# One transformer block on one core: the feed-forward part's residual stream, statistics and last product laid out with tokens on partitions

## The reference, cut to what matters

```python
xn = _layernorm(x, axis=-1)
x = x + _L0_attn_ref(xn, ...) + _L0_ffn_ref(xn, ...)
...
def _layer(x, wqkv, qs, ksc, wo, lg, lb, w1, b1, w2, b2):
    h = shift_token(x)          # second half of the channels from the token before
    q, k, v = split(h @ wqkv)   # 8 heads of 64; l2norm, scales, rotation
    o = local_attention(q, k, v)             # windows of 64, looks one window back
    x = x + o @ wo
    h = shift_token(x)
    mu = h.mean(-1, keepdims=True)
    var = h.var(-1, keepdims=True)
    h = (h - mu) / jnp.sqrt(var + 1e-05) * lg + lb
    h = h @ w1 + b1             # 128 -> 2 * 341
    a, g = jnp.split(h, 2, axis=-1)
    h = a * jax.nn.gelu(g, approximate=False)
    x = x + h @ w2 + b2         # 341 -> 128
    return x
```

## Time and profile before

| what | value |
|---|---|
| three runs, median (lowest to highest) | 379.59 us (376.76 to 379.63) |
| the profiled execution's own time | 379.34 us |
| its span, first to last instruction | 377.5 us |
| mean granted TensorE clock | 0.991 of full |
| busy: PE, ACT, DVE, POOL | 91%, 76%, 71%, 66% |
| instructions | 10808 |

### The profile page before, as it was taken

One profiled execution on the slowest core, in us unless ns is written; L12 is line 12 of the kernel. 1 busy time (PEld: TensorE's weight loads), 2 busy tenths in 40 slices (PEclk: granted clock), 3 DMA queues, 4 the chain that ended last, 5 costly groups with the idle time before them and its releaser, 6 DMA issues. The chain is left out here.

```text
span 377.5 us, 10808 instructions
## 1 busy us (share of the span) xinstructions
PE 344.2 (91%) x4015; PEld 264.3 (70%) x4015; DVE 268.9 (71%) x474; ACT 285.3 (76%) x881; POOL 250.5 (66%) x242
## 2 busy tenths in 40 slices
PE   1758779999999999998998989999999999999996
PEld 0557557888888888667565667778888887666565
DVE  4636677878887888657868767878887887565544
ACT  2746378998999899888635689989899989886321
POOL 2999479999989999821015778788989898320000
PEclk9999899999999999999999999999999999999999
DMA  6986032222232222270020322232223222200011
GB/s 201 372 158 184 5 126 56 65 68 55 65 71 66 51 64 65 65 259 16 9 56 0 71 69 67 52 76 58 56 61 79 58 65 61 55 7 16 20 36 56
DMA packets 35954, 28.68 MB, mean 76 GB/s; under 512 B 19221, under 2 KB 29375, under 8 KB 35391
## 3 DMA queue, kind: packets, MB, share of 16 engines
q1 hardware_dynamic: 35615, 27.54, 27.8%
q10 hardware_dynamic: 288, 0.46, 0.4%
HBM read 9.64 MB, written 1.05 MB: 28 GB/s over the span
## 5 line engine op out<-in xcount | busy, mean ns | idle before, releaser
L1204 ACT ACTIVATE probs<-ps,neg_max 128x128 f32<-128x128 f32 x256 | 90.1, 376 | 6.2 <-DVE neg_max L1438 5.4
L641 POOL TENSOR_TENSOR qkn<-work 128x512 f32<-128x512 f32 x64 | 80.6, 1281 | 12.3 <-DVE work L1384 9.2
L655 POOL TENSOR_TENSOR probs_n<-probs,row_inv 128x512 f32<-128x512 f32 x64 | 66.9, 1045 | 21.8 <-DVE row_inv L1443 19.9
L649 POOL TENSOR_TENSOR qkn<-qkn,rnorm 128x512 f32<-128x512 f32 x64 | 65.6, 1046 | 17.0 <-ACT rnorm L1160 16.5
L1204 ACT ACTIVATION_READ_ACCUMULATOR probs<-ps,neg_max 128x1 f32 x256 | 55.1, 215 | 0.0
L1153 ACT ACTIVATE work<-ps 128x1024 f32<-128x1024 f32 x32 | 32.8, 1026 | 18.2 <-issue 12.3
L1374 DVE TENSOR_REDUCE ss_pair<-work 128x16 f32<-128x1024 f32 x32 | 39.0, 1220 | 8.2 <-ACT work L1153 6.2
L166 PE MATMUL ps<-wqkv_hi,h_hi 128*128 128x512 f32 x96 | 42.5, 442 | 1.6 <-ACT work L1153 1.6
L1438 DVE TENSOR_REDUCE neg_max<-ps 128x4 f32<-128x512 f32 x64 | 41.0, 682 | 3.3 <-PE ps L865 3.3
L1384 DVE TENSOR_TENSOR work<-ps,cos_w 128x1024 f32<-128x1024 f32 x32 | 38.7, 1210 | 2.3 <-PE ps L168 2.3
L1384 DVE TENSOR_TENSOR work<-ps,sin_w 128x1024 f32<-128x1024 f32 x32 | 38.7, 1210 | 0.0
(11 more groups left out here) (156 smaller groups left out, 731.3 us busy)
## 6 DMA issues: line engine op xcount, KB each, us to landing
v_off<-v_tok SPq DMA_DIRECT2D x64, 128.0 KB, 2.3
k_t<-k_t SPq DMA_DIRECT2D x30, 128.0 KB, 2.3
cos_w<-in_cos_t SPq DMA_DIRECT2D x2, 1024.0 KB, 7.8
sin_w<-in_sin_t SPq DMA_DIRECT2D x2, 1024.0 KB, 10.7
x<-xin SPq DMA_DIRECT2D x16, 128.0 KB, 2.4
x_shift<-x SPq DMA_DIRECT2D x64, 32.0 KB, 1.8
x_raw<-in_x SPq DMA_DIRECT2D x4, 256.0 KB, 4.6
x_shift<-in_wqkv SPq DMA_DIRECT2D x1, 768.0 KB, 8.6
```

The lines of the kernel that those rows point to most:

```text
L641: pool.tensor_tensor(to, first, second[:, :, ::-1, :], ALU.add).then_inc(rot_summed, 1)
L649: pool.tensor_tensor(of, of, rnorm[:, part * HEADS:(part + 1) * HEADS].unsqueeze(2) .broadcast_to([P, HEADS, DH]), ALU.mult).then_inc(rot_ ...
L655: pool.tensor_tensor(probs_n[:, 4 * g:4 * g + 4, :], probs[:, 4 * g:4 * g + 4, :], row_inv[:, 4 * g:4 * g + 4].unsqueeze(2).broadcast_to([ ...
L1204: e = act.activation(probs[:, k, :], s_ps[g][:, cw * P:(cw + 1) * P], ACT.Exp, bias=neg_max[:, k:k + 1], accum_out=row_sum[:, k:k + 1])
```

## The change

The residual stream, the statistics and the result of the last product are laid out with tokens on partitions. `project_out` and `feed_out` swap their two operands, so that the products come out as 128 tokens by 128 channels. `feed_out` becomes 4 groups (`q`) of products with 128 moving columns, and `feed_out_last` likewise. `b2` and the patch branch's bias are two more rows of `w2` against rows of ones. The LayerNorm's shift is taken through `w1` once, at the front (`weigh_ln_shift`, 12 products with one moving column), and added to `b1` (`shift_biases`). `centered`, `variance`, `square`, `norm_rstd`, `normalize` on VectorE, `turn_out`, `turn_out_last`, `put_out` and `put_last` go.

In their place: `tile_stats` on VectorE (mean and variance of one tile), for tile t-3 as the last thing in each step t; `span_rstd` on ScalarE on 128x4 numbers, in steps 8 and 12 and twice later; `normalize_tile` on GpSimd for tiles 0 to 11 and `normalize_last` on VectorE for the last four; `turn_normalized` on TensorE (4 transposes per span); `round_normalized` on ScalarE, which applies the gain, and a shorter `split_normalized` on VectorE. Between the layers `turn_next` (4 transposes per span) is new, `round_turned` and `split_input` read PSUM, and those of spans 2 and 3 stand ahead of steps 1 and 2. The raw input is added on GpSimd (`add_raw`). `shift_x1` becomes three DMAs per tile, `shift_next` three per span. The load of `w1` goes to another buffer, and waits for the split of layer 0's `wqkv`.

```diff
@@ SP
 def shift_x1(n, t):
-    sp.dma_start(x1_shift[0:64, cols(t * P, P)], x1[0:64, cols(t * P, P)])
-    sp.dma_start(x1_shift[64:P, cols(t * P + 1, P)], x1[64:P, cols(t * P, P)])
+    sp.dma_start(hs[:, t, 0:DIM // 2], x1_tok[:, t, 0:DIM // 2])
+    sp.dma_start(hs[1:P, t, DIM // 2:], x1_tok[0:P - 1, t, DIM // 2:])
+    if t < TILES - 1:
+        sp.dma_start(hs[0:1, t + 1, DIM // 2:], x1_tok[P - 1:P, t, DIM // 2:])
...
-sp.wait_ge(xn_tr, SPANS)
+sp.wait_ge(wqkv_split, 1)
 sp.dma_start(w1_raw, w1.rearrange("l p n -> p l n"))
@@ GpSimd
+def normalize_tile(layer, t):
+    pool.wait_ge(ln_rstd_done, SPANS * layer + span_of(t) + 1)
+    pool.tensor_scalar(xn_tok[:, t, :], hs[:, t, :], mv[:, t, 0:1], rstd0[:, t:t + 1],
+                       ALU.subtract, ALU.mult)
...
     scale_rotated(n + 1)
+    if t == TILES - 1:
+        for tile in range(4, 8): normalize_tile(layer, tile)
     for g in range(2): normalize(n, g)
+    if t == TILES - 2:
+        for tile in range(4): normalize_tile(layer, tile)
+    if t == TILES - 1:
+        for tile in range(8, 12): normalize_tile(layer, tile)
@@ TensorE
 def feed_out(layer, j):
-    for c, (at, size) in enumerate(HID_PARTS):
-        pe.matmul(ffn_ps, w2_s[0:size, layer, c, :], hidden_of(layer, j, c)[0:size, :])
+    for q in range(4):
+        to = ffn_ps[:, q * P:(q + 1) * P]
+        for c in range(len(HID_PARTS)):
+            pe.matmul(to, hidden_of(layer, j, c)[0:rows, q * P:(q + 1) * P], w2_s[0:rows, layer, c, :])
...
 turn_patch_out(0)
+weigh_ln_shift()
 project_qk(0, 1)
...
 def step(t, parity):
+    if layer > 0 and t in (1, 2):
+        pe.wait_ge(v_evac, n + 1)
+        turn_next(t + 1)
     scores(n, parity)
     project_out(n - 2)
-    if t == TILES - 2: variance(0)
...
-    if t == TILES - 3: centered(0)
-    if t == TILES - 2: centered(1)
...
 scores(last, 1)
-centered(2)
 project_out(last - 2)
-variance(1)
+turn_normalized(0)
 weigh_values(last - 1, 0)
 gates(0, 0)
 turn_probs(last, 0, True)
 turn_probs(last, 1, True)
-variance(2)
 project_out(last - 1)
 gates(0, 1)
+turn_normalized(1)
 weigh_values(last, 1)
 project_out(last)
 gates(0, 2)
+turn_normalized(2)
 gates(1, 0)
-centered(3)
 gates(1, 1)
-variance(3)
 feed_out(layer, 0)
+gates(1, 2)
+gates(2, 0)
+turn_normalized(3)
+feed_out(layer, 1)
@@ ScalarE
 def step(t, parity):
+    if layer > 0 and t in (1, 2): round_turned(t + 1)
     exps(n, 0)
...
     inverse_norms(n + 2)
-    if layer > 0 and t in (1, 2): round_input(t + 1)
+    if t in (8, 12): span_rstd(t // 4 - 2)
@@ VectorE
+def tile_stats(t):
+    n = TILES * layer + t
+    dve.wait_ge(x1_shifted[t], (32 if t == 0 else 48) * (layer + 1))
+    dve.bn_stats(stats[:, t, :], hs[:, t, :]).then_inc(ln_stat_done, 1)
+    dve.wait_ge(ln_stat_done, n + 1)
+    dve.bn_aggr(mv[:, t, :], stats[:, t, :]).then_inc(ln_mv_done, 1)
...
 def step(t, parity):
+    if layer > 0 and t in (1, 2): split_input(t + 1)
     maxima(n, 0)
     maxima(n, 1)
...
     sum_squares(n + 2)
-    if layer > 0 and t in (2, 3): split_input(t)
-    if t == TILES - 2: normalize(0)
+    if there(t - 3): tile_stats(t - 3)
...
 add_out(layer, 0)
 hidden(1, 1)
+normalize_last()
+hidden(1, 2)
...
-    put_out(2)
     add_last(0)
     add_last(1)
-    put_last(0)
-    put_last(1)
```

More of the change, by code:

```diff
@@ L111, in pack_vectors @@
     rows = [b1.reshape(12, P), ffn_ln_g, ffn_ln_b, ffn_b2, np.reshape(attn_bout, (1, P))]
-    return np.concatenate([np.asarray(r) for r in rows], 0).T
+    columns = np.concatenate([np.asarray(r) for r in rows], 0).T
+    last = HID_PARTS[-1][1]
+    bias = np.zeros((P, LAYERS * P), np.float32)
+    bias[last] = np.reshape(ffn_b2, -1)
+    bias[last + 1, P:] = attn_bout
+    return np.concatenate([columns, bias], 1)
 def after(eng, sem, count):
@@ L666, in step @@
                         scale_rotated(n + 1)
+                    if t == TILES - 1:
+                        for tile in range(4, 8):
+                            normalize_tile(layer, tile)
                     if there(t):
@@ L669, in step @@
                             normalize(n, g)
+                    if t == TILES - 2:
+                        for tile in range(4):
+                            normalize_tile(layer, tile)
+                    if t == TILES - 1:
+                        for tile in range(8, 12):
+                            normalize_tile(layer, tile)
                     if layer == 0 and 2 <= t < 2 + 2 * LAYERS:
@@ L680, in _ @@
                 over_tiles(pool, step)
+                if layer == LAYERS - 1:
+                    for j in range(SPANS):
+                        add_raw(j)
                 if layer < LAYERS - 1:
@@ new lines, in feed_out_last @@
+                            pe.matmul(to, x_patch[:, (SPANS - 1) * WIDE + at:(SPANS - 1) * WIDE + at + P], a_wout_s[:],
+                                      start=True, stop=False)
+                            for c in range(len(HID_PARTS)):
+                                if half == 0 and q == 0:
+                                    pe.wait_ge(hh_done, 3 * jj + (c + 1))
+                                rows = hidden_rows(layer, c)
+                                mm = pe.matmul(to, hidden_of(layer, SPANS - 1, c)[0:rows, at:at + P],
+                                               w2_s[0:rows, layer, c, :], start=False, stop=(c == 2))
@@ L1047, in _ @@
                     pe.wait_ge(wqkv_split, 1 + NEXT_PARTS)
-                    pe.wait_ge(hn_scaled, SPANS * (layer + 1))
+                    pe.wait_ge(hn_split, SPANS * (layer + 1))
                     project_qk(layer + 1, last + 1)
-                    for c in range(3):
-                        gates(3, c)
+                    gates(3, 0)
+                    turn_next(1)
+                    gates(3, 1)
+                    gates(3, 2)
                     project_qk(layer + 1, last + 2)
@@ L1264, in step @@
                         round_next(t - NEXT_FIRST)
-                    if layer > 0 and t in (1, 2):
-                        round_input(t + 1)
+                    if t in (8, 12):
+                        span_rstd(t // 4 - 2)
                 over_tiles(act, step, TILES - 1)
@@ L1311, in _ @@
                     norms(last + 1)
+                    round_turned(1)
                 gelu(3, 1)
@@ L1480, in step @@
                 def step(t, parity):
                     n = t + layer * TILES
+                    if layer > 0 and t in (1, 2):
+                        split_input(t + 1)
                     if there(t):
```

395 lines of the change are left out of this document (181 added, 214 removed).

## The result

The kernel after takes 393.12 us (median of 4 runs, 390.86 to 395.98) against 379.13 for the kernel before in the same session: a ratio of 1.040, 95% interval 1.035 to 1.0455. I had forecast 380.4 and a range up to 386. The result lies outside the range, and in none of my rivals. Medians and ratios here are of the fast runs: one execution of v_behind (650 us) and one of the kernel before in the same session (1140 us) were slow ones. The profiled execution took 394.0 us, its span is 392.2, so 14.7 us more than the span of before.

A forecast was written before the change was run, and what follows sets the result against it. TensorE was taken to bound the feed-forward stretches, a ring through VectorE and ScalarE the attention steps; 379.3 + 6.5 + 0.3 + 2.3 - 2.3 - 6.2 + 0.5 + 0 = 380.4 us, range 375 to 386.

The forecast's parts named there:

- Part 1: Attention steps: statistics between sum_squares and maxima add 0.37 us to each of ten intervals a layer, +6.5; span_rstd adds +0.3.
- the ring: Attention steps: chain maxima, exponentials, invert, rotations, squares, sum_squares, next maxima sets 7.45 us; work added at its joint lengthens every step.
- Part 3: Last two steps of a layer: without centered and shorter work there, -0.75 and -1.5, so -2.25 us per layer.
- part 4: Feed-forward stretches: layer 1 -4.0 us; layer 0 0, as VectorE's tables make TensorE wait some 2.3 us; small products 0.111 apart.
- Part 2: Start of layer 1: maxima of steps 1 and 2 start 1.9 us later behind split_input, less 1.5 removed; +2.3 us.
- The rival with 399 us: Feed-forward last products: weight loads of small products, 0.19 us each, aren't hidden, adding 19 us; chance 0.03.
- the clock: Layer 0's feed-forward stretch: clock may fall after TensorE's 2.3 us idle time; half chance of 1 us, +0.5.
- Part 5: Front: weigh_ln_shift's 24 products, 2.6 us, fall where TensorE is idle; 0, bounds -0.5 and +3 us.
- Rival B: Feed-forward stretches: GpSimd normalizes tiles ahead of the last probabilities and TensorE waits, 2.6 us per layer; 385.6 us, chance 0.18.
- Rival C: Front takes its upper bound, with weigh_ln_shift's products at half clock throughout; 383.4 us, chance 0.10.

The follow-up runs named there:

- v_behind: split127, stats_early, turn_late and tables_early together, plus the v product behind the q and k transposes in layer 1's steps 1 and 2; ratio 0.9848 to the kernel before.
- stats_early: Kernel after with tile_stats(t-3) moved from behind sum_squares to behind residual(t-2), ahead of invert; 385.22 us.
- split127: Kernel after with the 127-row copy in shift_next cut into two, of 112 and 15 rows; 384.29 us.
- tiles_split: v_behind with the 127-row copies of single tiles in the steps also cut into 112 and 15 rows; 370.65 us, ratio 0.9796 to the kernel before.
- turn_late: split127 with turn_next, round_turned and split_input of layer 1's steps 1 and 2 moved behind scores, first exponentials and first invert; ratio that of split127.
- tables_early: split127 with three of the four scale_table moved to earlier places in layer 0's feed-forward stretch; 383.03 us.

## Why the prediction was wrong

By the stages of the table above, my sum had 0, +0.7, +0.5, +3.9 and -4.0, in all +1.1; the trace has +3.0, +0.9, +7.3, +6.1 and -2.6, in all +14.7.

**Part 1, right, by the ring.** Forecast +6.5 in the steps and +0.3. The intervals came out at 7.84 for 7.82, and the twenty of both layers are 7.0 us longer in all, for a forecast 6.8. Undoing the place alone gave 7.9 us in the medians and 6.4 in the steps (stats_early). The +0.3 is a slip of mine, four times 0.1 being 0.4; what shows of it is 0.2 us, in the interval of layer 0 behind step 8 (8.02 for 7.84).

**Part 3, right.** Forecast -2.25 per layer; the last two intervals of layer 1 are 7.85 and 6.90 against 8.58 and 8.53, -2.4.

**Part 1, wrong in one sentence, and part 4 with it: this is the step that failed.** "The shifted tile it reads was issued a whole step before; such a DMA of 256-byte rows lands in 2.3 us, so it isn't awaited." The row I took it from is of a copy over 128 partitions. I compared bytes and size of the rows, not the number of partitions. For the copies of one tile it did little harm: VectorE waits 0.92 us for one in each feed-forward stretch. But with the same belief part 4 priced the DMAs ahead of `turn_next` at nothing. The 127 rows of `shift_next`, with four times the descriptors, each cost 6.5 us of issue. Measured by split127: 8.8 us, two thirds of the miss. The trace of before has no copy from tile to tile over 127 partitions, all run over 64 or 128, so it couldn't show a transfer on one engine; the page of the Trainium skill could, and the diff had `1:P` in plain sight. With these 8.8 us the sum would have been 389.2, still 3.9 short of the result.

**Part 2, too small.** Forecast +2.3, and 0.37 more for the statistics of step 3: from 33.2 us to 35.9. Without the DMAs' share it is 37.2 (split127), 1.3 more. The first of the two late steps was 1.84 longer, for a forecast of 1.9. The second was 3.08 longer. I wrote that TensorE's transposes "are ready sooner". They aren't: they wait 0.69 us for `take_v` in step 1 and 1.42 in step 2, because of the shared bank, and the scores queue behind them. After the second wait these run at the lower clock (0.50 from 232 to 234 us):

```profile
231.00 1.11 PE L863 MATMUL ps<-small,shifted 128*128 128x128 f32 x4 [1.42 <-ACT v_tok L1220]
232.05 0.64 PE L920 MATMUL ps<-masks 64*64 64x512 bf16 x4
232.47 1.92 PE L926 MATMUL ps<-k_t,q_t 64*64 64x128 f32 x32
```

These are TensorE's lines in split127. I had looked for what waits behind the added work on VectorE only, not at the queue of TensorE.

**Part 4, right in its mechanism, too large in its gain.** The small products run at the forecast spacing: in the trace of after the four groups of six of `feed_out` start at 187.89, 188.55, 189.22 and 189.89, 0.67 for six products, 0.111 each. The rival with 399 us and the Trainium skill's spacing rule are thereby excluded for these float32 products. The tables did make TensorE late, 2.51 us for 2.3. But of the -4.3 us that `centered` and `variance` give back, TensorE now spends a part waiting for the last exponentials, whose bank the first `gates` need: 1.61 us of idle time ahead of it in layer 0 and 1.39 in layer 1. The same two lines of the kernel before, where TensorE had `variance` to fill the time:

```profile
171.01 0.47 PE L166 MATMUL ps<-hn_hi,w_hi 128*128 128x512 f32 x1 [0.54 <-DVE hn_lo L1478]
...
333.76 0.47 PE L166 MATMUL ps<-hn_hi,w_hi 128*128 128x512 f32 x1 [0.66 <-DVE hn_lo L1478]
```

With 1.1 and 0.7 us lost again so, layer 0's stretch without the DMA is +0.9 (split127) for a forecast 0 and 0.5 for the clock, and layer 1's end -2.6 for -4.0; the other 0.7 of the latter I have not traced. My -1.7 by TensorE's count in layer 0 left out the split product's +0.4; the sum didn't use it. Which work could fill this gap wasn't tried.

**Part 5, on the low side.** Forecast 0, bounds -0.5 and +3; 1.1 us on average over eleven executions. The other 0.8 us of the +3.0 in the profiled pair stood ahead of these products already.

**Rival B** (normalizing ahead of the last probabilities) cost nothing that can be seen: the turns of these stand right behind the first `gates`. **Rival C** (the front at its bound of +3) was half true: the products cost up to 2.2 us.

The terms that were missing or too small, 8.8 for the DMA, 1.3 in part 2, 1.1 in the front, 0.9 and 1.4 in part 4, make 13.5 us, or 13.0 less the 0.5 that the sum had for the clock, for a miss of 12.7. They come from single traces and from medians of different sessions, so the agreement is no closer than the 3 us or so of the medians. The clock has a share in several of them: in its four executions the kernel after was granted 0.97 to 0.98, the kernel before 0.99 to 1.00, and tiles_split 0.99 to 1.00 again. How much of this is cause and how much effect of the waits was not tested.

## What to carry to other kernels

For each DMA that a change adds, read its partition count first: if it is a prime such as 127 or 113, cut it so that most of the rows go by sixteens (112 and 15 here), and look at what is queued behind it, not only at who waits for its data. Where an instruction is added to a queue, its place counts for more than its duration: the same two statistics cost 7 us in the joint of a ring and almost nothing behind the residual sum, 1.4 us after the start of `maxima`. And where a buffer is shared, write down the whole round trip (here v, copy, turn, round, split, v); in turn_late moving one call of it only moved the wait, while v_behind, which put other work in front of the waiting product, took 3.15 us off.

## Behaviour of the hardware that I had not expected

- The issue of a DMA lasted 6.53 to 6.57 us (four of four) behind one with 508 rows of 256 bytes on one engine, 5.67 to 5.80 behind one with 452, 0.9 to 1.0 behind one with 448 that sixteen share, and 0.86 (the median) behind one with 127.
- Beside GpSimd a product on VectorE took twice as long. VectorE's lines of tables_early, then GpSimd's at the same time:

```profile
173.12 2.62 DVE L1421 TENSOR_TENSOR cos_w<-cos_w,qk_scale 128x1024 f32<-128x1024 f32 x1
...
176.49 1.24 DVE L1421 TENSOR_TENSOR cos_w<-cos_w,qk_scale 128x1024 f32<-128x1024 f32 x1
```
```profile
172.57 2.06 POOL L665 TENSOR_TENSOR probs_n<-probs,row_inv 128x512 f32<-128x512 f32 x2
174.59 6.27 POOL L672 TENSOR_SCALAR xn_tok<-shifted,mv,rstd 128x128 f32<-128x128 f32 x4
```

  It ended 1.1 us after GpSimd's two, in all four kernels that have it there (2.57 to 2.62 us; 1.2 to 1.4 elsewhere), as if it had begun only then. GpSimd waits in turn: three of its next four `tensor_scalar` overlap one of VectorE's table products and last 1.8 to 1.9 us each, the fourth 0.8, and the four take 6.27 us, where the same four take 3.12 in the kernel after. The Trainium skill ("SBUF — State Buffer", section "SBUF: two separate sides") says that an operation of VectorE with both inputs in SBUF and one of GpSimd that reads SBUF lock each other out for the whole instruction; these rows agree, and tables_early gained its 2.25 us in spite of it.
- The granted clock isn't the same from one execution to the next in the same place. In the front, 24 one-column products took 2.45 us in six of eleven profiled executions, and 2.60, 2.93, 3.00, 3.19 and 3.56 us in the others. In layer 0's feed-forward stretch TensorE waits 2.5 us for `hidden(1, 1)` in the kernel after and in split127 alike. Behind this wait the clock is at its lower level in the first and stays up in the second, as these windows show, one of each kernel, 1.4 us after the wait's end:

```profile
196.00:198.00 2.00, 2.00 (x8) 1.62 (x7) 0.59 (x2) 0.69 (x1) 0.00 (x0) 0.50 0.07 15
```
```profile
192.00:194.00 2.00, 2.00 (x20) 1.91 (x19) 1.53 (x3) 0.97 (x2) 0.00 (x0) 1.00 0.30 62
```

  The first does 8 matmuls in its 2 us, the second 20. I had given this +0.5 us, at even chances.
